# Bias rows of two experts on GpSimd, expert 2 mixed in one late pass, and the first gate ahead of Q's split

## What is computed

```python
xn = _layernorm(x, axis=-1)
logits = xn @ router_w + router_b + load_balancer
rw, sel = top_k(logits, 2); rw = softmax(rw)
e0 = silu(xn @ sw_w1) * (xn @ sw_w3) @ sw_w2
e1 = gelu(sym @ me_c1w + me_c1b) @ me_c2w + me_c2b      # sym is linear in xn
e2 = h2 @ ce_gen_w + ce_gen_b                           # h2: norm, relu layer, norm
e3 = gelu(xn @ ml_w1 + ml_b1) @ ml_w2 + ml_b2
out = x + attention(xn) + sum of rw * (chosen experts)
```

## Time and profile before

| what | us |
|---|---|
| median of 3 runs | 451.15 |
| lowest and highest run | 451.05, 454.04 |
| span of the profiled execution, first to last instruction | 449.1 |
| PE, DVE, ACT, POOL busy in it | 438.6, 402.5, 271.4, 245.8 |

### The profile page before, as it was taken

How to read it: one execution, slowest core, us unless ns; L and a number is a source line. 1 busy time by engine, 2 the same in 40 slices (tenths; PEclk the granted TensorE clock), 3 DMA queues, 4 the chain that set the end, 5 groups by cost and what they waited for, 6 DMA issues and landing times.

```text
span 449.1 us, 9603 instructions
## 1 busy us (share of the span) xinstructions
PE 438.6 (98%) x2804; PEld 371.8 (83%) x2804; DVE 402.5 (90%) x1344; ACT 271.4 (60%) x535; POOL 245.8 (55%) x366
## 2 busy tenths in 40 slices
PE   4999999999999999999999999999999999999997
PEld 3778888788888888888888988888888888888886
DVE  4887989989899898989989899898989989898897
ACT  4965838557384764838556484755838566483841
POOL 3893727557273664727466272664727466372451
PEclk9999999999999999999999999999999999999999
DMA  7522123032130412223032130413123031220201
GB/s 261 38 72 72 25 63 78 26 93 47 51 70 23 105 35 70 47 70 70 23 93 47 55 62 23 113 27 89 27 70 70 23 99 41 58 58 16 58 0 48
DMA packets 86484, 27.18 MB, mean 61 GB/s; under 512 B 64993, under 2 KB 82113, under 8 KB 86465
## 3 DMA queue, kind: packets, MB, share of 16 engines
q1 hardware_dynamic: 86176, 26.94, 25.0%
q10 hardware_dynamic: 288, 0.01, 0.0%
HBM read 14.66 MB, written 12.06 MB: 60 GB/s over the span
## 4 chain that ended last, share of the span: by engine, by line
PE 94%; DVE 3%; DMA 1%; issue 0%; DVEq 0%; ACT 0%; SPq 0%
PE S L1133 14%; PE S L1135 13%; PE S L1134 13%; PE EX L1059 12%; PE EX L1079 6%; PE S L1223 3%; PE S L1218 3%; PE S L1219 3%; PE EX L1087 3%; PE TR L1173 2%; PE S L1231 2%; PE S L1230 2%; PE S L1229 2%; PE S L1148 2%; PE S L1147 2%; PE S L1146 2%
## 5 line engine op out<-in xcount | busy, mean ns | idle before, releaser
L486 POOL TENSOR_TENSOR hid3l<-hid,hid3h 128x512 fp32r<-128x512 f32 x64 | 80.3, 1287 | 29.3 <-ACT hid3h L599 29.3
L1133 PE MATMUL S<-xh,WH 128*128 128x512 f32 x224 | 90.4, 403 | 0.0
L1135 PE MATMUL S<-xh,WL 128*128 128x512 f32 x224 | 88.4, 394 | 0.0
L1134 PE MATMUL S<-xl,WH 128*128 128x512 f32 x224 | 88.1, 393 | 0.0
L444 POOL TENSOR_TENSOR veps_x<-mv_x,eps 128x4 f32<-128x4 f32 x16 | 3.2, 200 | 111.7 <-DVE mv_x L643 111.7
L1059 PEld LDWEIGHTS EX<-scaled,hid 128*128 128x128 f32 x480 | 55.9, 192 | 1.2
L1059 PE MATMUL EX<-scaled,hid 128*128 128x128 f32 x480 | 56.0, 275 | 0.0
L1133 PEld LDWEIGHTS S<-xh,WH 128*128 128x128 f32 x224 | 42.2, 188 | 14.1 <-DVE hid L822 3.1
L1135 PEld LDWEIGHTS S<-xh,WL 128*128 128x128 f32 x224 | 42.1, 188 | 9.9
L573 ACT COPY kv<-S 128x64 f32<-128x64 f32 x64 | 13.6, 213 | 60.3 <-PE S L1148 54.6
L1134 PEld LDWEIGHTS S<-xl,WH 128*128 128x128 f32 x224 | 42.3, 189 | 8.0
(11 more groups left out here) (201 smaller groups left out, 1066.4 us busy)
## 6 DMA issues: line engine op xcount, KB each, us to landing
X<-x SPq DMA_DIRECT2D x16, 256.0 KB, 2.8
turning<-xn SPq DMA_DIRECT2D x15, 256.0 KB, 2.6
xb<-turning SPq DMA_DIRECT2D x60, 64.0 KB, 2.6
turning<-e3T SPq DMA_DIRECT2D x15, 256.0 KB, 2.4
e3b<-turning SPq DMA_DIRECT2D x60, 64.0 KB, 2.6
out<-OUT SPq DMA_DIRECT2D x15, 256.0 KB, 2.4
W<-weights SPq DMA_DIRECT2D x1, 768.0 KB, 8.2
W<-weights SPq DMA_DIRECT2D x1, 512.0 KB, 5.8
```

What stands on the lines that cost most here:

```text
L486: pool.tensor_tensor(hid3l[:, j, :], hid[3][:, j, :], hid3h[:, j, :], ALU.subtract) \
L1133: pe.matmul(bank[:, :], wh, hi, start=True, stop=False)
L1134: pe.matmul(bank[:, :], wh, lo, start=False, stop=False)
L1135: pe.matmul(bank[:, :], wl, hi, start=False, stop=True).then_inc(unit_ready, 1)
```

## The change

Three things. On POOL, after its low halves and ahead of `norm_x`, a new step `add_biases` multiplies the bias row of expert 1 and that of expert 2 by the group's weights, adds the two, and adds the sum into `OUT`: four operations on 128x512 elements with two drains between. DVE's step for expert 1's bias row (L926) goes, and so does the one for `gen_bias` in the tail (L949). Expert 0's mixing now waits for POOL's `biases_added`. On DVE, `coef` is made right behind the third gate, since POOL needs it. Expert 2's two passes (L762, L771) become one from its bank, with a weight `coef_r` = coef times rstd, behind the fourth gate and `turn_next`. And the first gate, `silu(0)`, stands ahead of the subtraction of Q's low half.

```diff
@@ -217,7 +217,7 @@
 
 
         pr = sb("pr", [P, NT, P])
-        e2 = sb("e2", [P, NT, P])
+        bias1, bias2 = (sb(name, [P, NT, P]) for name in ("bias1", "bias2"))
         gate = sb("gate", [P, 4, T])
 
         S = [ctx.enter_context(nc.psum_tensor(f"S{b}", [P, T], F32)) for b in range(BANKS)]
@@ -391,7 +391,7 @@
                 swap(g, e3b, e3T, turning[1], e3_kept, e3_swapped)
 
             def store(g):
-                sp.wait_ge(out_ready, g.count(1, 1))
+                sp.wait_ge(ex_taken[3], g.count(1, 1))
                 sp.dma_start(out[g.index()].rearrange("(t p) h -> p t h", p=P), OUT[g.par][:, :, :]) \
                     .then_inc(out_stored[g.par], DMA_INC)
 
@@ -489,8 +489,27 @@
                 for j in range(2):
                     pool.tensor_tensor(hidl[:, j, :], hid[2][:, j, :], hidh[:, j, :], ALU.subtract) \
                         .then_inc(hid_low, 1)
+                add_biases(g, first)
                 if two_more(g):
                     norm_x(Group(g.pair, g.off + 2))
+
+            def add_biases(g, first):
+
+                if first:
+                    pool.wait_ge(bias_rows_loaded, 2 * DMA_INC)
+                    pool.wait_ge(setup_took, TAKEN.index("gen_b") + 1)
+                pool.wait_ge(att_added, g.count(1, 1))
+                pool.wait_ge(route_step, g.count(ROUTE_STEPS, ROUTE_STEPS))
+                wide = [P, NT, P]
+                pool.tensor_tensor(bias1[:, :, :], row("me_c2b").unsqueeze(1).broadcast_to(wide),
+                                   coef[g.par][:, :, 1:2].broadcast_to(wide), ALU.mult)
+                pool.tensor_tensor(bias2[:, :, :], gen_bias[:, :].unsqueeze(1).broadcast_to(wide),
+                                   coef[g.par][:, :, 2:3].broadcast_to(wide), ALU.mult)
+                pool.drain()
+                pool.tensor_tensor(bias1[:, :, :], bias1[:, :, :], bias2[:, :, :], ALU.add)
+                pool.drain()
+                ins = pool.tensor_tensor(OUT[g.par][:, :, :], OUT[g.par][:, :, :], bias1[:, :, :], ALU.add)
+                ins.then_inc(biases_added, 1)
 
             def root_u(g):
 
@@ -754,27 +773,21 @@
                                                    op0=ALU.mult, op1=ALU.add)
                 ins.then_inc(ex_taken[e], 1)
 
-            def expert2_scale(g):
+            def expert2(g):
 
                 dve.wait_ge(u_rstd, g.count(1, 1))
+                dve.tensor_tensor(coef_r[:, :], coef[g.par][:, :, 2], rstd["u"][:, :], ALU.mult).then_inc(u_scaled, 1)
+                dve.wait_ge(u_scaled, g.count(1, 1))
                 dve.wait_ge(ex_ready[2], g.count(1, 1))
-                for t in range(NT):
-                    ins = dve.scalar_tensor_tensor(out=e2[:, t, :], in0=EX[EX_BANK[2]][:, t, :],
-                                                   scalar=rstd["u"][:, t:t + 1], in1=gen_bias[:, :],
+                dve.wait_ge(ex_taken[1], g.count(1, 1))
+                for t in range(NT):
+                    ins = dve.scalar_tensor_tensor(out=OUT[g.par][:, t, :], in0=EX[EX_BANK[2]][:, t, :],
+                                                   scalar=coef_r[:, t:t + 1], in1=OUT[g.par][:, t, :],
                                                    op0=ALU.mult, op1=ALU.add)
                 ins.then_inc(ex_taken[2], 1)
 
-            def expert2_add(g):
-                dve.wait_ge(ex_taken[2], g.count(1, 1))
-                dve.wait_ge(ex_taken[3], g.count(1, 1))
-                for t in range(NT):
-                    ins = dve.scalar_tensor_tensor(out=OUT[g.par][:, t, :], in0=e2[:, t, :],
-                                                   scalar=coef[g.par][:, t, 2:3], in1=OUT[g.par][:, t, :],
-                                                   op0=ALU.mult, op1=ALU.add)
-                ins.then_inc(out_ready, 1)
-
             def expert0(g):
-                mix(g, 0, bias1_added)
+                mix(g, 0, biases_added)
 
             def expert1(g):
                 mix(g, 1, ex_taken[0])
@@ -852,11 +865,11 @@
                 for t in range(NT):
                     ins = dve.bn_aggr(mv["c"][:, t, :], stats["c"][:, t, :])
                 ins.then_inc(c_stats, 1)
-                dve.wait_ge(qk_high, g.count(2, 1))
-                dve.tensor_tensor(Q[C:2 * C, :], qk_bank[C:2 * C, :], Q[C:2 * C, :], ALU.subtract)
                 silu(0)
                 if not first:
                     u_combine(g.prev())
+                dve.wait_ge(qk_high, g.count(2, 1))
+                dve.tensor_tensor(Q[C:2 * C, :], qk_bank[C:2 * C, :], Q[C:2 * C, :], ALU.subtract)
                 dve.wait_ge(qk_high, g.count(2, 2))
                 dve.tensor_tensor(K[2 * C:3 * C, :], qk_bank[3 * C:4 * C, :], K[C:2 * C, :], ALU.subtract) \
                     .then_inc(qk_split, 1)
@@ -897,59 +910,45 @@
                                          scalar=-0.5, in1=logit, op0=ALU.mult, op1=ALU.add).then_inc(lean_ready, 1)
                 route(dve.tensor_scalar(half[:, :, :], rank, 1.5, 0.5, ALU.is_lt, ALU.mult))
 
-                if not first:
-                    expert2_scale(g.prev())
                 wait(dve, out_stored[g.par], g.half(DMA_INC, 0))
                 dve.wait_ge(att_ready, g.count(1, 1))
                 dve.tensor_tensor(OUT[g.par][:, :, :], ATT[:, :, :], X[g.par][:, :, :], ALU.add) \
                     .then_inc(att_added, 1)
                 silu(2)
+                dve.wait_ge(tlean_ready, g.count(1, 1))
+                route(dve.scalar_tensor_tensor(out=coef[g.par][:, :, :], in0=tlean[:, :, :], scalar=1.0,
+                                               in1=half[:, :, :], op0=ALU.add, op1=ALU.mult))
                 if first:
                     fold_last()
                 silu(3)
                 if not first and not last:
                     turn_next(g)
                 if not first:
+                    expert2(g.prev())
                     wait(dve, ex_taken[3], g.prev().count(1, 0))
                     dve.wait_ge(e3_swapped, g.prev().count(SWAPS * DMA_INC, SWAPS * DMA_INC))
                     dve.transpose(e3t[:, :, :].rearrange("p t n -> p (t n)"), e3b[:, :, :].rearrange("p t n -> p (t n)")) \
                         .then_inc(ex_ready[3], 1)
-                dve.wait_ge(tlean_ready, g.count(1, 1))
-                route(dve.scalar_tensor_tensor(out=coef[g.par][:, :, :], in0=tlean[:, :, :], scalar=1.0,
-                                               in1=half[:, :, :], op0=ALU.add, op1=ALU.mult))
                 if first:
                     turn_next(g)
                 if not first:
-                    mix(g.prev(), 3, ex_taken[1], src=e3t)
-                dve.wait_ge(att_added, g.count(1, 1))
-                for t in range(NT):
-                    ins = dve.scalar_tensor_tensor(out=OUT[g.par][:, t, :], in0=row("me_c2b"),
-                                                   scalar=coef[g.par][:, t, 1:2], in1=OUT[g.par][:, t, :],
-                                                   op0=ALU.mult, op1=ALU.add)
-                ins.then_inc(bias1_added, 1)
+                    mix(g.prev(), 3, ex_taken[2], src=e3t)
                 f2, free = unit("f2")
                 dve.scalar_tensor_tensor(out=u[:, :], in0=f2[:, :], scalar=vec("f2b"), in1=h2[:, :],
                                          op0=ALU.add, op1=ALU.add).then_inc(free, 1)
                 if not last:
                     x_low(g.next())
-                if not first:
-                    expert2_add(g.prev())
                 if two_more(g):
                     x_moments(Group(g.pair, g.off + 2))
                 if last:
-                    mix(g, 3, bias1_added)
+                    mix(g, 3, biases_added)
                 assert rs[0] == ROUTE_STEPS
 
             def tail(g):
 
                 u_moments(g)
                 u_combine(g)
-                dve.wait_ge(ex_taken[3], g.count(1, 1))
-                for t in range(NT):
-                    ins = dve.scalar_tensor_tensor(out=OUT[g.par][:, t, :], in0=gen_bias[:, :],
-                                                   scalar=coef[g.par][:, t, 2:3], in1=OUT[g.par][:, t, :],
-                                                   op0=ALU.mult, op1=ALU.add)
-                ins.then_inc(last_step, 1)
+
                 def zero(t):
 
                     dve.wait_ge(last_zero, t + 1)
@@ -957,23 +956,23 @@
                                              scalar=coef[g.par][:, t, 0:1], in1=OUT[g.par][:, t, :],
                                              op0=ALU.mult, op1=ALU.add).then_inc(last_step, 1)
 
-                dve.wait_ge(last_step, 1)
+                dve.wait_ge(ex_taken[3], g.count(1, 1))
                 zero(0)
                 zero(1)
                 dve.wait_ge(u_rstd, g.count(1, 1))
                 dve.tensor_tensor(coef_r[:, :], coef[g.par][:, :, 2], rstd["u"][:, :], ALU.mult).then_inc(last_step, 1)
                 dve.wait_ge(ex_ready[2], g.count(1, 1))
-                dve.wait_ge(last_step, 4)
+                dve.wait_ge(last_step, 3)
```

(12 more changed lines are left out.)

## The result

The changed kernel takes 455.45 us as the median of six runs (454.07 to 459.21) against 451.19 us (451.05 to 454.04), a ratio of 1.010 with a 95% interval of 1.0062 to 1.0138. I had forecast 462.0, so +11 where +4.3 was measured: the sign held, the size did not. One fact is needed to read these numbers: three of the six runs show a mean granted TensorE clock of 1.000 (454.07, 454.65, 454.67), the others 0.996 (456.22, 457.70, 459.21), and every run of the kernel before shows 0.999 or more. So there are two costs: about 3 us of work that is late, most of it in turn 0 and in the last turn, and in half of the runs a clock that falls.

What follows compares the result with a forecast made beforehand. PE, busy 98% of the span, was taken to bound the kernel. Loop stops of +8.7 us and +2.7 for last turn and tail gave +11.4, so 462.5, stated as 462.0 us; range 450.0 to 469.

Steps and rivals of the forecast that it cites:

- step 3: DVE instructions with two SBUF inputs and POOL operations hold each other up each turn; x-normalisation starts 1.40 us late.
- step 2: POOL's four added 128x512 operations a turn take 1.26 us each, with two drains 5.35 us, inside a 7.8 us hole.
- Cheap: Rival: held, but POOL operations take 1.03 us; x-normalisation 0.48 late, inside the slack; 452 us, chance 0.15.
- dear: Rival: POOL's operations with broadcast input take 1.55 us each, in 13 turns and the tail; 478 us, chance 0.12.
- step 3's end: Late x-normalisation stops PE before the `n` transposes by 0.67 us in each of turns 1 to 13: +8.7 us.
- The slack, 0.73: In the loop, how late the x-normalisation may start before PE stops: 0.63 us on POOL plus 0.1 at PE's transposes.
- step 4: First gate ahead of Q's split frees a bank 0.69 us sooner; taken as 0, at best 0.9 us over 15 turns.
- There POOL's work holds no additions of DVE: Turn 0 has no group before it to mix, so it was left out of the 13 turns that lose time.
- step 5: Last turn has no expert 0 ahead of `u`'s transposes, so expert 3 ending at 440.8 delays `u`: +2.9 us.
- The tail's -0.2: The tail loses the 1.1 us `gen_bias` step, but `rstd_u` behind it is quicker by only 0.18 us: -0.2 us.

Runs made afterwards that it cites:

- e10: The changed kernel with POOL's two products reading plain 128x512 inputs of zeros instead of broadcast ones, both bias rows missing from the output: 463.65 us, ratio 1.0263.
- e3: The changed kernel without POOL's four 128x512 operations and drains, one 128x4 operation signalling instead, bias rows missing from the output: 452.21 us, ratio 1.0011.
- e8: The changed kernel with POOL's four operations replaced by two 128x4 operations around eight 128x512 memsets, bias rows missing: 452.3 us, ratio 1.0023.
- e6: The changed kernel with one more 128x512 POOL sum, into a tensor nobody reads, ahead of POOL's last addition: 471.31 us, ratio 1.0426.
- e9: The changed kernel with 18 unread 128x128 products on PE in the last turn, while it waits for `u`: 456.98 us, ratio 1.0108.
- e4: The changed kernel with `u` made right behind expert 2 in the last turn, ahead of expert 3's additions: 452.72 us, ratio 1.0031.
- e5: The changed kernel with last-turn `u` right behind expert 2, and in turn 0 Q's split before the first gate and `coef` behind the fourth: 451.95 us, ratio 1.0017.

## Why the prediction was off

**Holding (step 3): right.** `coef` 0.81 and 0.73, expert 3's additions 1.92 and 1.96, the order of events as worked out. `coef_r`, which I had held in each turn, is held only in the last; in the loop it falls into the drain. It changes nothing behind it, since expert 3 is held anyway.

**POOL's operations (step 2), with the additions behind them (step 3): the step that failed.** The mechanism was right, the two terms were too large. I priced "128x512, two inputs" at 1.26 each, and kept 1.03 as the lower bound. The additions took 1.29 and 1.28, the two products with broadcast inputs 1.05. From the end of the low halves (247.29) to that of the last addition (252.31) are 5.02 us, I had 5.52. Further, the additions of expert 3 end 0.95 after POOL (253.26 against 252.31) and the next instruction, `u`, starts 0.87 after it, where I had counted 1.06. So the x-normalisation stands 0.71 us later against PE's `u` transposes (by the timelines 255.83 against 255.35; before 254.08 against 254.31), instead of 1.40.

The rivals had the same flaw. "Cheap" and "dear" each put one price on all four operations, though only the two products have broadcast inputs. What came is a case between: two at 1.05 and two at 1.28.

**PE's stop in the loop (step 3's end): +8.7 forecast, +0.24 measured.** The slack, 0.73, was right: a lateness of 0.71 just fits, and e10, some 0.50 later, adds 0.50 a turn. It was a sum just above a threshold: 0.69 us too much of lateness became 0.67 us in each of 13 turns. I had named this case ("held, but POOL cheap", 452) and given it 0.15; its mechanism is the one that came, with dearer additions and two costs outside it.

**The gate (step 4): right,** 0.2 to 0.35 us where I took 0 and bounded it at 0.9. But I followed it only in the loop; in turn 0, where the first gate waits 0.72 us for its activation, it costs 0.68.

**Turn 0: missed.** "There POOL's work holds no additions of DVE" is true, yet POOL's old low halves hold the moved `coef`, 1.98 us, ahead of work that PE waits for: 0.32. With the gate's 0.68 that is +1.00.

**The last turn (step 5): +2.9 forecast, +2.2 measured,** short by the same 0.46 of the products and 0.19 of the additions. I had put nearly all of it down to POOL's chain; by e3 POOL's four operations make 1.41 of it, and 0.80 is there without them. The tail's -0.2 was -0.1.

**The clock: missed.** Six of 12 runs of the changed kernel lose more after the stop. By the low runs alone the change costs 454.07 - 451.05 = 3.0 us, as the spans say; the medians say 4.3.

Sum as measured: 1.00 + 0.24 + 2.21 - 0.25 = +3.2 of span, and the remaining 1 us or so of the median from the clock.

## What to carry to other kernels

Where a sum ends near a threshold that repeats every turn (here 0.7 us of slack), the forecast is the chance of crossing it, not a value: price the cheap bound of each unknown operation through the whole chain, and give that case a chance of its size. Work moved from VectorE to GpSimd is not free even in GpSimd's longest hole: look which VectorE instructions there read two SBUF tensors, and follow any moved instruction into the written-out first and last turns, where the cover of the loop is missing. A PE stop of 2 us close to the end can cost again through the clock.

## What the runs showed of the hardware

- What happens where two GpSimd instructions follow without a drain is not the same each time. In turn 0 `coef` began in the first subtraction (30.87 to about 32.1) and came out only behind the second: 1.98 us in the changed kernel, 1.98 in e3 and e8 too. In e6 one addition got in at the boundary and the next was held. The section of the Trainium skill named above says that whoever issues first gets the shared pair for the whole instruction (it says so of VectorE's two-port modes). The second addition of e6 agrees, held for one whole POOL addition; the 1.98 us go beyond it, and no run here tells why. In a drain of some 0.15 us a short one gets in (`coef_r`, 0.14 at 249.38).
- GpSimd's 128x512 product of fp32 takes 1.05 us with broadcast inputs and 1.30 with plain ones; eight memsets of that size take 3.79, 0.47 from one to the next.
- The granted clock fell to near 0.5, for some 3.4 us, behind PE stops of 3.12 us (e6) and 2.60 us (e10), in 4 of 4 runs each, and in 6 of 12 runs, by their mean of 0.996, with one of 2.06. That it is the same stretch in those runs is inferred, since their profile was not the one kept; the 1.4 us that such a run takes longer fit. With a stop of 0.63 (e3) it was 0 of 12 runs, and with PE busy instead (e9) or not stopped (e4, e5) 0 of 30.
